# First attention layer: a head's rows gathered into one tile of 64 rows, maxima placed by transfers; in the block, the values' bias added to the heads

## What is computed

```python
def _L0_xattn_ref(x, mask, kv, kv_mask, Wq, bq, Wk, bk, Wv, bv):
    q = einsum('oc,bct->bot', Wq, x) + bq          # k, v alike, of kv
    attn = softmax(where(kv_mask, q*scale @ k, -inf))     # 16 heads, 512 x 512 each
    mean = attn @ v;  ex2 = attn @ (v*v)
    std = sqrt(relu(ex2 - mean*mean))
    return (masked_instance_norm(x) * std + mean) * mask

def _L1_xattn_ref(hidden, encoder, ...):
    x = hidden + attention(split(ln1(hidden) @ w_qkv + b_qkv)) @ w_ao + b_ao
    x = x + attention(ln2(x) @ w_q + b_q, encoder @ w_kv + b_kv) @ w_co + b_co
    return x + gelu(ln3(x) @ w1 + b1) @ w2 + b2
```

## Time and profile before

| | |
|---|---|
| time, median of three runs | 1775.89 us (1771.3, 1775.89, 1777.62) |
| time of the profiled execution | 1772.35 us |
| its span | 1770.6 us |
| PE busy | 1671.6 us, 94% |
| DVE busy | 1293.5 us, 73% |
| ACT busy | 1046.9 us, 59% |
| granted TensorE clock, mean of the span | 0.98 |

### The profile page before, as it was taken

One profiled execution on the slowest core, in us unless ns is written; L12 is line 12 of the kernel. 1 busy time (PEld: TensorE's weight loads), 2 busy tenths in 40 slices (PEclk: granted clock), 3 DMA queues, 4 the chain that ended last, 5 costly groups with the idle time before them and its releaser, 6 DMA issues.

```text
span 1770.6 us, 32725 instructions
## 1 busy us (share of the span) xinstructions
PE 1671.6 (94%) x11645; PEld 1143.2 (65%) x11645; DVE 1293.5 (73%) x2790; ACT 1046.9 (59%) x2319; POOL 341.3 (19%) x435
## 2 busy tenths in 40 slices
PE   5999999999999998899999989999999899999999
PEld 3434333333433345788878777788878688888888
DVE  1677888888888757899999999999999872323222
ACT  1456666667666666777767777777777641121111
POOL 0002121312213132233222222233222120000000
PEclk7999999999999998999999999999999899999999
DMA  6344453544534422223233524333333330000000
GB/s 231 114 139 148 151 183 103 165 143 150 174 120 136 157 75 83 67 73 78 68 100 75 144 60 121 90 91 94 94 88 86 101 114 0 24 0 21 4 24 13
DMA packets 110512, 172.79 MB, mean 98 GB/s; under 512 B 23184, under 2 KB 38928, under 8 KB 110224
## 3 DMA queue, kind: packets, MB, share of 16 engines
q1 hardware_dynamic: 98768, 145.52, 27.6%
q0 software_dynamic: 9472, 20.99, 4.6%
q10 hardware_dynamic: 2112, 4.19, 0.7%
HBM read 72.58 MB, written 39.32 MB: 63 GB/s over the span
## 4 chain that ended last, share of the span: by engine, by line
PE 56%; DVE 28%; issue 7%; ACT 6%; DMA 2%; SPq 1%; POOL 0%; ACTq 0%; DVEq 0%; POOLq 0%
PE ps L480 10%; PE ps L1884 9%; PE ps L1858 7%; PE ps L453 6%; DVE at_t L1337 5%; DVE at_t L1342 5%; PE ps L1208 4%; DVE nmax L556 3%; PE ps L1218 3%; PE ps L465 3%; PE ps L427 2%; PE ps L1157 2%; PE ps L1863 2%; PE ps L1146 1%; DVE at_probT L1486 1%
## 5 line engine op out<-in xcount | busy, mean ns | idle before, releaser
L556 DVE TENSOR_REDUCE nmax<-ps 128x2 f32<-128x1024 f32 x256 | 310.0, 1219 | 135.3 <-PE ps L453 134.0
L730 ACT ACTIVATE prob<-ps 128x1024 f32<-128x1024 f32 x256 | 262.1, 1024 | 166.9 <-PE ps L465 163.7
L1556 ACT ACTIVATE at_prob<-at_t,at_nmax 128x256 f32<-128x256 f32 x512 | 256.6, 505 | 110.0 <-DVE at_nmax L1342 97.1
L480 PE MATMUL ps<-prob,v 128*64 128x512 f32 x1024 | 276.1, 618 | 0.0
L1342 DVE CUSTOM_DVE_ANT_0 at_t<-at_t,at_off 128x256 f32<-128x256 f32 x512 | 232.3, 490 | 8.8
L453 PE MATMUL ps<-ring 32*128 32x512 f32 x1024 | 194.4, 451 | 31.4 <-DMA ring<-rows 16.3
L453 PEld LDWEIGHTS ps<-ring 32*128 32x128 f32 x1024 | 86.1, 184 | 177.7 <-issue 126.4
L2043 DVE CAST mlp_h_hi<-mlp_h 128x512 fp32r<-128x512 f32 x64 | 28.4, 443 | 212.7 <-ACT mlp_h L1955 180.1
L1702 POOL TENSOR_TENSOR at_low<-at_low,at_high 128x512 fp32r<-128x512 f32 x64 | 86.2, 1347 | 478.9 <-DVE at_high L1371 478.9
L1955 ACT ACTIVATE mlp_h<-ps,b 128x512 f32<-128x512 f32 x48 | 33.1, 690 | 218.5 <-PE ps L1858 218.5
L1157 PE MATMUL ps<-ident,at_prob 128*128 128x128 f32 x1024 | 158.7, 278 | 0.0
(11 more groups left out here) (220 smaller groups left out, 3891.1 us busy)
## 6 DMA issues: line engine op xcount, KB each, us to landing
ring<-rows SPq DMA_DIRECT2D x64, 512.0 KB, 4.9
rows<-shares_of SPq DMA_DIRECT2D x96, 256.0 KB
at_k_stack<-at_high SPq DMA_DIRECT2D x256, 64.0 KB, 2.4
rows<-far SPq DMA_DIRECT2D x8, 1024.0 KB, 7.2
at_q_stack<-at_high SPq DMA_DIRECT2D x128, 64.0 KB, 2.7
at_q_stack<-at_high POOLq DMA_DIRECT2D x128, 64.0 KB, 2.4
at_q_stack<-at_low SPq DMA_DIRECT2D x128, 64.0 KB, 2.1
at_k_stack<-at_low POOLq DMA_DIRECT2D x128, 64.0 KB, 2.3
```

The lines of the kernel that those rows point to most:

```text
L480: mm = eng.matmul(ps[2 * QD * k:2 * QD * (k + 1), VB, :], v[:, c, HG * G + 2 * p + k, :], prob[:, M % PROBS, k, :], start=(c == 0), stop=( ...
L556: eng.tensor_reduce(nmax[:, n % 2, j, 2 * p:2 * p + 2], ps[:, at:at + 2, :], AX, ALU.max, negate=True).then_inc(s_max, 1)
L730: eng.activation(prob[:, M % PROBS, :, :], ps[:, ST:ST + 2, :], ACT.Exp, scale=float(HD0) ** -0.5).then_inc(s_exp, 1)
L1556: ins = eng.activation(prob[:, m % 2, i, :], t[:, p, i, :], ACT.Exp, scale=-1.0, bias=nmax[:, m % 4, i:i + 1], accum_out=z[:, T % 2, j, 2 ...
```

## The change

**Rows.** A head's rows of q stand in one tile of 64 partitions, and so do those of k; a group's four heads take two tiles of 64 partitions by two places (`q_rows`, `k_rows`). `scores` and `turned` are two matmuls of 64 rows in place of four of 32, without halves. The constant rows (32 to 47) of a slot are written by two transfers of 16 rows by 64 sets (`constants_out`), and only `rows_in` waits for them.

**Maxima.** `spread_maxima` writes eight columns of `wide` per 128 queries; the item "turn" is L442's four matmuls alone, at step 1 in place of 2; ACT copies eight rows to `top`; and `tops_in`, on the SP queue behind `regroup(2n)`, places them with four transfers of two rows (4 KB) into the ring's slot. The first `turned` of a group waits for these (`s_top`). `q2m` is gone.

**Order.** The items of "q" are at steps 2 and 3 of even groups (before 3, 4), of "k" at 5 and 6 (before 6, 7); `high_of` and `rest_of` follow at 4 and 7. At the start, the first group's rows go out and in by themselves ahead of the second's (`rows_out(..., (0,))`, `first_rows_in`), and `ident`, `wv` and `bv` are loaded behind them; `row`, `b0` and the first mask bits are loaded from ACT's queue.

**Block.** `values` is a plain copy on ACT. The bias of the values is added to the finished heads: `high_heads` has it as its bias, and `low_heads` becomes a SCALAR_TENSOR_TENSOR. `b_self` and `b_cross` hold one row each.

```diff
-        if s in (3, 4, 6, 7) and w % 2 == 0 and w // 2 + 1 < PAIRS:
-            return [("q" if s < 5 else "k", w // 2 + 1, (s % 3,))]
-        if s == 2 and 0 <= w - 1 < GROUPS:
+        if s in (2, 3, 5, 6) and w % 2 == 0 and w // 2 + 1 < PAIRS:
+            return [("q" if s < 4 else "k", w // 2 + 1, ((s + 1) % 3,))]
+        if s == turn_step(w) and 0 <= w - 1 < GROUPS:
             return [("turn", w - 1, (0, 1))]
...
+        def constants_out(k, src, done):
+
+            for i in range(2):
+                eng.dma_start(d["rows0"][k].rearrange("s p (i r) t -> i r (s p) t", i=2)[i, CONST:CONST + HD0],
+                              src[ROWS * i + CONST:ROWS * i + CONST + HD0, None, :].broadcast_to([HD0, 2 * RING, D]))\
+                   .then_inc(done, DMA)
...
+        def first_rows_in(name, p):
+
+            k = "qk".index(name)
+            eng.wait_ge(s_first_out[name], 3 * DMA)
+            constants_written(name, 0)
+            eng.dma_start(ring[:, 0, 2 * k + p, :].bitcast(F32), d["rows0"][k, 0, p]).then_inc(s_first_in[p], DMA)
...
+        def tops_in(n):
+
+            taken(eng, "turn", n)
+            for h in range(HG):
+                at = ROWS * (h % 2) + CONST + 1
+                eng.dma_start(q_rows[at:at + 2, n % RING, h // 2, :].bitcast(F32),
+                              top[2 * h:2 * h + 2, n % 2, :].bitcast(F32)).then_inc(s_top, DMA)
...
+        constants_out(0, scrap, s_const)
         far_out(0)
+        rows_out("k", 0, (0,))
+        rows_out("q", 0, (0,))
+        for p in range(2):
+            first_rows_in("k", p)
+            first_rows_in("q", p)
+        eng.dma_start(ident[:], d["ident"]).then_inc(s_ident, DMA)
         eng.dma_start(w0[:, :, 2 * S:], d["w0"][:, :, 2 * S:]).then_inc(s_wv, DMA)
         eng.dma_start(bv0[:], d["bv0"]).then_inc(s_wv, DMA)
-        eng.dma_start(ident[:], d["ident"]).then_inc(s_ident, DMA)
-        rows_out("k", 0)
-        rows_in("k", 0)
-        rows_out("q", 0)
-        rows_in("q", 0)
+        rows_out("k", 0, (1,))
+        rows_out("q", 0, (1,))
...
                 regroup(2 * n)
+            if 0 <= w - 1 < GROUPS:
+                tops_in(w - 1)
             lead(w, False)
...
-                eng.matmul(bank, ident_r[:], q2[:, n % RING, :], start=True, stop=False)
                 for j in range(DC):
-                    mm = eng.matmul(bank[:, P * j:P * (j + 1)], wide[:, j, :], ident_r[:], start=False,
-                                    stop=(j == DC - 1))
+                    mm = eng.matmul(bank[:, P * j:P * (j + 1)], wide[:, j, :], ident_r[:], start=True, stop=True)
...
+        def scores(N):
 
             n, j, p = N // 8, N % 4, N % 8 // 4
             for i in range(2):
-                r = rows_of(2 * p + i)
-                lhsT, rhs = (q1, k1) if half == 0 else (q2, k2)
...
+                r = rows_of(i)
+                mm = eng.matmul(ps[:, SC + 2 * (N % 2) + i, :], q_rows[r, n % RING, p, P * j:P * (j + 1)],
+                                k_rows[r, n % RING, p, :], start=True, stop=True)
+            mm.then_inc(s_score, 1)
...
                     if M % 8 == 0:
-                        taken(eng, "turn", M // 8)
+                        eng.wait_ge(s_top, HG * DMA * (M // 8 + 1))
...
-            eng.activation(q2m[:, n % 2, :], ps[:, MB, :], ACT.Copy).then_inc(s_free, 1)
+                eng.wait_ge(s_top, HG * DMA * (n - 1))
+            eng.activation(top[0:2 * HG, n % 2, :], ps[0:2 * HG, MB, :], ACT.Copy).then_inc(s_free, 1)
...
-            eng.activation(h_hi[:, G, :], h_raw[:, G % 2, :], ACT.Copy).then_inc(s_hhi, 1)
+            eng.activation(h_hi[:, G, :], h_raw[:, G % 2, :], ACT.Identity,
+                           bias=g["b_feat"][:, 4 + run // NB, G:G + 1]).then_inc(s_hhi, 1)
+
+        def values(run, n):
+            made(eng, "v", n, run)
+            if run >= 2:
+                eng.wait_ge(s_pv, UNITS * (run - 1))
+            eng.activation(v[:, run % 2, n, :], ps[:, IB, :], ACT.Copy).then_inc(s_free, 1)
```

More of the change, by code:

```diff
@@ new lines, in rows_out, with constants_written @@
+            src = shares_of[ROWS * slots[0]:ROWS * (slots[-1] + 1), k, :, :]
+            for part, row in ((0, 0), (0, 48), (1, 16)) if name == "q" else ((0, 0), (0, 16), (1, 48)):
+                eng.dma_start(d["rows0"][k, at].rearrange("s p (i r) t -> (s p i) r t", r=ROWS)[:, row:row + HD0, :],
+                              src[:, part, :].bitcast(F32))\
+                   .then_inc((s_first_out if m == 0 and slots == (0,) else s_out)[name], DMA)
+        def constants_written(name, n):
+            if name == "q":
+                eng.wait_ge(s_const, 2 * DMA)
+            else:
+                eng.wait_ge(s_far_out, 2 * DMA * (n // NG + 1))
@@ L1520, in runs @@
                             inverse_roots(n, m - 9)
-                    if m in (11, 13) and run + 1 < RUNS:
-                        values(run + 1, m // 2 - 5)
                     if m % 4 == 2 and m > 2:
@@ L1676, in runs @@
                         widen(run, (m - 1) // 4)
+                    if m in (11, 13) and run + 1 < RUNS:
+                        values(run + 1, m // 2 - 5)
                     if m in (5, 6) and NB <= run + 1 < RUNS:
```

181 lines of the change are left out of this document (86 added, 95 removed).

## The result

The changed kernel takes 1809.55 us (median of four, 1805.06 to 1822.05) where the kernel before takes 1776.76: a ratio of 1.0189, interval 1.0163 to 1.0215. It is slower by 33 us. The forecast was 1765 and the range ended at 1791.

What follows compares the result with a forecast made beforehand. It took PE's loop with ACT (1.85 us per plain step) and the SP queue's chain as the limits. Start -9, pairs +4, last groups +2 and block -8 made -11 from 1775.89: 1765, range 1738 to 1791.

Steps and rivals of the forecast that it cites:

- the price of `tops_in`: SP queue, first layer: four issues at 0.43, 1.9 us in all, lengthening odd parts by 1.5 per pair on average.
- terms of pairs, tail and first odd group: First layer: +4 us for 14 pairs, +2 for the last three groups' open waits, 2 back in the first odd group.
- the even part: PE, ACT and DVE's stretch of each pair in the first layer: about 1.2 us shorter, subtracted from the odd part's growth.
- the items one step earlier: Even groups of the first layer: q and k items moved forward, a gain of 0.4 us, between 0 and 0.8.
- C, the clock: Rival, first layer: TensorE's clock falls in new gaps, up to +24 us over 14 odd groups, put at 1785; chance 0.19.
- B, the queue doesn't bind: Rival, first layer: SP queue does not limit, so PE's gain is kept, -29 in place of +4, 1732; chance 0.14.
- The plain step: First-layer step without an extra item: from 1.85 us, set by the loop with ACT, to PE's 1.67, 0.18 gained.
- D: Rival: tiles of 64 rows do not run two at a time, 0.46 more per step, +118 us, 1883; chance 0.04.
- The start: Before the first maximum: reordered and halved first transfers bring it 10 to 11 us earlier; -9 after 2 back, between -13 and -4.
- The block: Block after the first layer: values moved from DVE to ACT, -8 us, between -14 and +2.
- Rival E: The block gives nothing, as ACT's copies delay exponentials PE waits for: -3 in place of -11, 1773; chance 0.16.

Runs made afterwards that it cites:

- run with filling: Changed kernel with extra matmuls, result not used, in TensorE's waits ahead of odd groups' first turned products and even groups' first scores: 1815.59 us, ratio 1.0215.
- before_four: Kernel before with four more two-row transfers on the SP queue at the place of the maxima's, nobody waiting for them: 1810.32 us, ratio 1.0194.
- no_tops: Changed kernel without the four transfers of the maxima and the wait for them, maximum not subtracted: 1772.81 us, ratio 0.9975.
- no_tops_k_first: Changed kernel without the maxima's transfers and their wait, and with rows_out of k at the head of odd groups' queue work: 1741.8 us, ratio 0.9798.
- tops_aside: Changed kernel with the same four transfers sent to unused rows and no wait of TensorE for them, maximum not subtracted: 1824.73 us, ratio 1.0265.
- block_only: Kernel before with only the block's part of the change (values on ACT, bias at the heads): 1774.96 us, ratio 0.999.

## Why the prediction was wrong

**The step that failed is the price of `tops_in` and what it does to the chain.** The working had four issues at 0.43, 1.9 in all, and +0.3 per pair. Measured are 2.5 to 2.8 for four (0.62 each, 2.48 in most groups), and from the first to the last maximum +43.5 us where the terms of pairs, tail and first odd group made +8. Per pair it is +3.0 where +0.3 was put: the odd groups +3.2 in place of 1.5, the even ones -0.2 in place of -1.2. Even with every term at its worst bound the sum would have been 1796. It failed in three places:

1. *The duration.* 0.62 and not 0.43, the upper end of its bounds (2.6). I took the row that was smallest in bytes as the nearest. That is 0.6 to 0.9 per odd group, 8 to 13 us in all; with 2.6 for the issues and 0.9 for the even part the working itself gave +17.
2. *The rest of the chain was held fixed.* Of the 5.3 in group 15 only 3.0 are the new issues. `rows_out` of q ended 1.0 us into group 15 before and ends 3.0 into it now, since the even group got 1.2 shorter and the queue's work in it did not (it even has the four issues more). `regroup` then starts later, runs into the rows still in flight and takes 1.1 more, and the landing of k's rows 0.6 more.
3. *The even part's gain was subtracted from the chain.* -1.2 is there in groups 14 and 26. Groups 10, 18 and 22 lost it to the clock (19.2 to 19.3, and 17.9 in the run with filling, which keeps the clock full there). Groups 12, 16, 20 stayed at 19.6 (before 19.5, 19.6, 19.8): there DVE has its burst, and PE stands at the item of k, which needs the bank that `rest_of` of q frees. In group 12, PE's timeline:

```profile
278.12 0.50 PE L478 MATMUL ps<-c_hi,w_hi 128*128 128x512 f32 x1 [1.69 <-DVE shares_of L591]
```

PE waits 8.8 us for these in six groups (8, 12, 16 and so on); in the kernel before there is no such wait. So the items one step earlier, costed at a gain of 0.4, meet a wait that the working didn't have; whether the earlier step or the shorter steps bring it wasn't tried. And a gain on PE ahead of a chain that begins with work of the queue is only had if the queue keeps up.

before_four shows the price of the four issues without the new tiles: in the kernel before they cost 33 us. They are not all of the +43.5 in the changed kernel's first layer: without the transfers it still takes 607.1 us from the first to the last maximum (no_tops), 14 more than before, since `regroup` and the rows by themselves are last on the shorter even groups, with the clock's stretches behind; with `rows_out` of k moved ahead it is 576.2 (no_tops_k_first). By these runs the transfers made about 30 of the 43.5, and the rest of the chain, which the working held fixed, the other 14.

**C, the clock**, named the right event and the wrong price. It does fall: the changed kernel has 11 stretches of 3.4 us at half the clock (1.2 GHz) in groups 7 to 27, behind waits of 1.7 to 3.9 us, the kernel before none there. One of them, in group 15:

```profile
334.75:338.16 3.41, 3.41 (x12) 0.79 (x8) 1.24 (x2) 2.27 (x3) 0.00 (x0) 0.50 0.64 180
```

But it counted 1.7 for each where PE is last, and inside the odd groups PE is not last: with the clock full the group kept its length. At the head of an even group it costs near what was said: 1.3 to 1.4 each in groups 10, 18 and 22, and 3.15 in group 12 of tops_aside, for two stretches. Its border between waits of 1.83 and 1.92 didn't hold either: here the clock fell behind waits of 1.67 and 1.69 (groups 13 and 25) and stayed full behind one of 2.29 (the head of group 4).

**B, the queue doesn't bind**, was worked out as 1732; with the queue out of the way and no maxima sent, 1741.8 was measured. The totals are close, the parts are not. The plain step fell to 1.67 as worked out, and groups without DVE's burst gained what was put (even ones 17.9 to 18.2 in place of 18.4 to 19.1, most odd ones 16.3 to 17.4 in place of 17.5 to 19.1). But groups 8, 12, 16 and so on got longer (20.2 to 21.8 in place of 18.9 to 20.1), with a stretch at half the clock behind the wait for `rest_of` in five of the six. Between the first scores of groups 2 and 31 that leaves 12 us of the 29 that B put for the pairs; start and block give 13, and the ends of the first layer most of the rest. **D** fell: two tiles of 64 rows run together, 0.34 and 0.33.

**The start** gave 6.2 and not 9 to 11. Each issue of a half transfer took 1.15 where 0.6 was put (6.87 for six), and each read 1.3 where 0.4 was put; the first scores came at 26.47, and `ident` (copied at 28.47) was only just not late. The rule of the Trainium skill ("DMA: Bandwidth & Descriptors", "Rules for kernel authors") that halves aren't worth it gave a start of -5; the run with whole transfers says that halves bring 1.35 us here. The measurement decides, and it is close to the rule: most of the 6.2 is the order, not the cut.

**The block** gave 6.1 in the trace of the change and 3.9 in that of block_only, where 8 was put. PE's waits for `at_v`, 6.9 us in one line of before and 21.0 over all lines, are gone: what is left of them in the block of the changed kernel is

```profile
PEld ps L1251 <- ACT at_v L1639: 0.2, 1, 0.2
```

while ACT's copies took 0.588 each. Rival E is right in part: in the block PE's waits for ACT's exponentials, in the line where they are largest, rose from 22.7 to 25.4 us, and those of its weight loads there from 43.6 to 47.7. It is less than what the waits for `at_v` gave back, and the block is shorter all the same.

## What to carry over

A queue that issues transfers in order is an engine like the others: when work is added to it, cost it by the number of issues. Their price doesn't go by bytes (here 0.38 us for 512 KB in one read, 0.43 for 2 KB, 0.62 for 4 KB, 0.64 for 256 KB), so until a new one is measured take the dearest that is there. Then follow the whole loop around it, since what slips past a group's end delays the next group's head. Before a gain on the compute engines is booked, ask which chain ends the group; here the same change that came with a loss of 33 us shows a gain of 36 once the chain and the four transfers are out of the way (in a kernel that leaves out the subtraction of the maximum). The cheapest test of such a cost is the kernel before with the new transfers and nobody waiting for them.

## What the runs showed of the hardware

- Issuing a transfer of 4 KB from SBUF to SBUF took 0.62 us on the SP queue and the same on ACT's (2.48 and 2.50 for four), as much as one of 256 KB (0.64).
- A 4 KB transfer landed 1.2 us behind its last issue with nothing large in flight, and 4.3 us behind it with 768 KB under way from another queue. So here a small transfer landed later beside large ones of another queue. Both hold in every odd group of the two traces where the rows stood so: 1.1 to 1.2, and 4.1 to 4.3.
- Six issues in a row slowed to 1.15 and 1.39 us each at the start, behind the writes of the constants; in group 15 one issue of `regroup` took 1.75 behind 768 KB of rows. Three issues of 256 KB that had waited for the constants to land took 2.03, 0.68 each. So an issue isn't of fixed cost when data ahead of it hasn't landed; by what mechanism wasn't tried.
- After waits of 1.67 to 3.9 us on TensorE, 12 stretches of 3.4 us at half the clock came in the changed kernel; other waits of 1.69, 1.81 and 2.29 were followed by none. Inside a group whose end another chain set, a stretch cost nothing (23.08 us at a mean of 0.93, 23.03 at 1.00); at the head of one that TensorE set, 1.3 to 1.4 us.
